# The head loop of a GroupNorm + attention kernel, rolled or written out

## What is computed

```python
def _gn(v, G=32, eps=1e-5):
    g = v.reshape(B_, G, C_ // G, H_, W_)
    m = jnp.mean(g, axis=(2, 3, 4), keepdims=True)
    s = jnp.var(g, axis=(2, 3, 4), keepdims=True)
    return ((g - m) / jnp.sqrt(s + eps)).reshape(v.shape)

def attention(x, Wq, Wk, Wv, Wp):            # HEADS = 12, dh = 64, N = H * W = 1024
    q, k, v = (jnp.einsum('oc,bchw->bohw', W, x).reshape(B, 12, 64, N) for W in (Wq, Wk, Wv))
    attn = jax.nn.softmax(jnp.einsum('bhdn,bhdm->bhnm', q, k) / 8, axis=-1)
    out = jnp.einsum('bhnm,bhdm->bhdn', attn, v).reshape(B, C, H, W)
    return jnp.einsum('oc,bchw->bohw', Wp, out)

x = x + attention(_gn(x), Wq, Wk, Wv, Wp)
```

## Time and profile before

| | |
|---|---|
| median of 3 runs | 3445.78 us (3442.05 to 3448.36) |
| the profiled execution | 3443.71 us |
| its span, first to last instruction | 3441.9 us |
| mean granted TensorE clock | 0.994 of full speed |
| instructions in the profile | 51849 |

### The profile page before, as it was taken

The page is one execution under the profiler, slowest core; times in us unless marked ns, Lnnn a source line. Parts: engine busy times, 40 slices in busy tenths (PEclk is TensorE's granted clock), DMA queues, the critical chain, the costliest instruction groups (busy, mean ns, idle before and its releaser), DMA issues.

```text
span 3441.9 us, 51849 instructions
## 1 busy us (share of the span) xinstructions
PE 3363.1 (98%) x18656; PEld 2257.7 (66%) x18656; DVE 1480.4 (43%) x1980; ACT 1116.3 (32%) x1992; POOL 1848.6 (54%) x795
## 2 busy tenths in 40 slices
PE   6999999999999979999999999999999999999999
PEld 5898888889888855445555555555555555555557
DVE  5332333233233145555444454444544545444431
ACT  3111111111111115554444444434444434444441
POOL 4000000000000029998888888888888888888883
PEclk9999999999999989999999999999999999999999
DMA  6332433423243332334434434434344334344434
GB/s 213 113 138 97 146 114 136 146 104 136 100 143 110 109 148 87 124 117 154 160 115 154 143 107 160 155 130 157 115 160 160 114 134 148 124 160 135 148 106 178
DMA packets 246840, 464.52 MB, mean 135 GB/s; under 512 B 47584, under 2 KB 97632, under 8 KB 245344
## 3 DMA queue, kind: packets, MB, share of 16 engines
q1 hardware_dynamic: 246624, 461.66, 38.7%
HBM read 260.11 MB, written 200.67 MB: 134 GB/s over the span
## 4 chain that ended last, share of the span: by engine, by line
PE 59%; issue 2%; DMA 1%; DVE 1%; SPq 1%; ACT 0%; POOL 0%; ACTq 0%; DVEq 0%; POOLq 0%
PE psum L754 20%; PE psum L767 19%; PE psum L786 10%; PE psum L737 7%; PE psum L849 1%; PE psum L777 1%; DVE half_max L930 1%; DMA out<-y 1%; DMA top<-turned 0%; ACT p_all L883 0%; SPq L570 0%; DMA k<-k_parts 0%; DVE flipped L940 0%; POOL sums L710 0%; DMA compact<-total 0%
## 5 line engine op out<-in xcount | busy, mean ns | idle before, releaser
L710 POOL TENSOR_TENSOR sums<-sums,p_all 128x1024 f32<-128x1024 f32 x576 | 1354.1, 2384 | 71.5 <-ACT p_all L883 71.3
L930 DVE TENSOR_REDUCE half_max<-psum 128x2 f32<-128x1024 f32 x768 | 939.5, 1225 | 645.7 <-PE psum L737 641.1
L883 ACT ACTIVATE p_all<-psum 128x512 f32<-128x512 f32 x1536 | 793.3, 602 | 919.6 <-PE psum L754 882.4
L767 PE MATMUL psum<-p_all,v 128*64 128x512 f32 x3072 | 743.4, 605 | 0.0
L754 PE MATMUL psum<-q,k 64*128 64x512 f32 x4608 | 667.4, 394 | 8.3 <-DMA top<-turned 5.8
L718 POOL TENSOR_TENSOR wp<-sums,wp 128x1536 fp32r<-128x1536 f32 x1 | 3.4, 3445 | 1177.6 <-ACT wp L916 1177.6
L754 PEld LDWEIGHTS psum<-q,k 64*128 64x128 f32 x4608 | 426.1, 185 | 120.3 <-ACT p_all L883 33.1
L240 PE MATMUL psum<-xn_hi,w_hi 128*128 128x512 f32 x1128 | 440.4, 390 | 7.0 <-DVE stage L377 7.0
L240 PE MATMUL psum<-xn_hi,w_lo 128*128 128x512 f32 x1128 | 439.5, 390 | 0.0
L240 PE MATMUL psum<-xn_lo,w_hi 128*128 128x512 f32 x1128 | 439.5, 390 | 0.0
L290 ACT CAST stage<-psum 128x512 fp32r<-128x512 f32 x192 | 112.6, 588 | 968.0 <-PE psum L240 962.5
(11 more groups left out here) (75 smaller groups left out, 2350.7 us busy)
## 6 DMA issues: line engine op xcount, KB each, us to landing
q_parts<-stage SPq DMA_DIRECT2D x192, 256.0 KB, 2.2
k_parts<-stage SPq DMA_DIRECT2D x192, 256.0 KB, 2.3
q<-q_parts SPq DMA_DIRECT2D x48, 1024.0 KB, 6.8
k<-k_parts SPq DMA_DIRECT2D x48, 1024.0 KB, 8.9
a<-o_parts SPq DMA_DIRECT2D x84, 512.0 KB, 7.9
v_rows<-stage SPq DMA_DIRECT2D x128, 192.0 KB, 2.1
v<-v_rows SPq DMA_DIRECT2D x48, 512.0 KB, 4.2
recip_all<-recip_rows SPq DMA_DIRECT2D x96, 256.0 KB, 3.8
```

What stands on the lines that cost most here:

```text
L710: pool.tensor_tensor(sums[:, m % 2, i, :], first, p_all[:, i, n, :], ALU.add).then_inc(added, 1)
L767: mm = pe.matmul(heads[part, h, :], v[:, e, t, part], p_all[:, i, (m * MT + t) % EXPS, cols], start=(t == 0), stop=(t == MT - 1))
L883: act.activation(p_all[:, i, (m * MT + t) % EXPS, h * BANK:(h + 1) * BANK], psum[:, SCORE_BANKS[2 * h + i], :], ACT.Exp, scale=SCALE).then ...
L930: dve.tensor_reduce(half_max[:, :, t, h], of, AX.X, ALU.max, negate=True).then_inc(max_done, 1)
```

## The change

Both places that run the pairs lose the hardware loop, and all 48 pairs are written out, on all engines. In the pairs 12 to 41 p becomes a number, as it is already in the others; each engine's program for them becomes five times as long. The loads, the stores, the matmuls, their order and their buffers are the same.

```diff
@@ -410,7 +410,6 @@
     BODY = KT
     SHIFT = 2
     LAG = KT + SHIFT
-    PEELED = 2 * BODY
     SCALE = float(DH) ** -0.5
@@ -514,12 +513,7 @@
 
         def all_pairs(eng, pair):
 
-            for p in range(PEELED):
-                pair(p, p % BODY, None)
-            with eng.Fori(PEELED // BODY, NP // BODY - 1) as u:
-                for m in range(BODY):
-                    pair(u * BODY + m, m, u)
-            for p in range(NP - BODY, NP):
+            for p in range(NP):
                 pair(p, p % BODY, None)
 
         def at_least(p, n):
@@ -652,12 +646,7 @@
             sp.wait_ge(set_done, SETS)
             maxima(0, 0)
             sp.wait_ge(wp_lo_done, len(wp_raw))
-            for p in range(PEELED):
-                pair(p, p % BODY, p // KT)
-            with sp.Fori(PEELED // BODY, B - 1) as b:
-                for m in range(BODY):
-                    pair(b * KT + m, m, b)
-            for p in range(NP - BODY, NP):
+            for p in range(NP):
                 pair(p, p % BODY, p // KT)
```

## The result

The changed kernel takes 3438.94 us (median of 22 runs, 3436.77 to 3440.63), the kernel before 3445.68 us (22 runs, 3441.52 to 3451.07). The ratio is 0.998 with a 95% interval of 0.9973 to 0.9986. That is 6.7 us less, just inside the bound of 0.2%, and the runs are closer together: 3.9 us from the lowest to the highest, where the kernel before has 9.5. The profiled execution took 3439.11 us with a span of 3437.3, 4.6 us less than the one before.

The account below looks back on a forecast made before the run. TensorE (PE), busy 98% of the span, was taken to bound the kernel. -8.25 + 3.0 = -5.25 us gave 3438.5 from the profiled 3443.71; with half of the median's extra 2.1 us, 3439.5 us, range 3433.5 to 3444.5.

Parts of the forecast that it names:

- Term 1: Pairs 12 to 41: the loop's four jumps back go, all of their cost on PE's path, -8.25 us.
- Term 2: ScalarE's exponents: the loop's quicker waits are lost, 0.10 us a pair over 30 pairs, +3.0 us (bounds +2.1 and +3.6).
- Term 3: Instruction queues: fetching the written-out code is not more than the loop's and costs nothing further.
- The half of 2.1 us: Median over profiled run: 2.1 us, some perhaps jump stalls that go as well; half was taken as saved.
- (a): Rival, the loop's jumps: larger in ordinary runs, 11.6 us, so -8.6 us and faster by over 0.2%; chance 0.36.
- (b): Rival, block boundaries on PE or SP: reading code in a line stalls, +18.6 us, 3457 us, slower; chance 0.05.
- (c): Rival, the jumps' place in the batch: jumps cost next to nothing, stalls stay, +3.0 us, 3446.7 us; chance 0.04.

Follow-up runs that it names:

- experiment 1: The changed kernel, but with TensorE alone keeping the loop and the other engines written out: 3444.45 us, ratio 1.0002 to the kernel before.
- experiment 2: The changed kernel, but with SyncE alone keeping the loop and the other engines written out: 3440.3 us, ratio 0.9992 to the kernel before.
- experiment 3: The kernel before with 24 pairs written out ahead of the loop in place of 12, so two jumps instead of four: 3440.08 us, ratio 0.999.
- changed_again: The changed kernel as it is, run again in a later batch as a yardstick: 3438.54 us, ratio 0.998 to the kernel before.
- project_straight: The changed kernel with the projection phase written out as well, so no loop is left: 3438.81 us, ratio 0.9981 to the kernel before.
- experiment 7: The changed kernel with the projection phase's loop at two batches per turn (3451.34 us, ratio 1.0022), or with that phase written out (3438.81 us, ratio 0.9981).

## Why the prediction was right

**Term 1** (the jumps, 8.25 us, all on PE's path) held in both its parts, and the runs separate them: PE's own jump 5.6 us in four pieces (experiment 1), SP's jump through the q and k loads, the store of y and the gathers, 0.7 us in that profile and 2.1 in the kernel before (experiment 2). Halving the jumps halved the pieces (experiment 3). The 0.7 us that the term put down to slower matmuls behind a pause is not shown by itself: with TensorE's jumps alone the 30 pairs take 1357.73 us, 5.80 more than in the changed kernel, which is its pieces of 5.6 and 0.2 more.

**Term 2** was mis-sized a little: 45.05 to 44.95 us a pair was forecast, +3.0 us; measured 45.06, +3.4 (1351.93 - 1348.5), inside its bounds of 2.1 and 3.6. Its cause, read from one product and one exponent, is confirmed from four sides: moving one wait brings 44.99 back in the written-out code, moving it makes the loop slower, keeping only ScalarE's loop gives 44.98, and the idle time ahead of line 743 shows it (3.2, 0.7 with ScalarE looped). That cause is 2.3 to 2.5 of the 3.4 us (1351.93 less 1349.67 or 1349.43). The rest, about 1 us or 0.03 a pair, no experiment brought back, and its cause stays open.

**Term 3** (transfer of the code costs nothing) held, and more than held: 64 blocks instead of 78.

**The sum.** Forecast -5.25 from profile to profile, measured 3443.71 - 3439.11 = -4.60; over the 30 pairs alone it is 1356.75 - 1351.93 = -4.82, 0.43 short, which is term 2. Forecast for the median 3439.5, measured 3438.94. The half of 2.1 us that I gave to stalls in ordinary runs was too little: the medians are 6.7 us apart in the kernels' own runs, and 4.8 in the batch of `changed_again` (3443.3 - 3438.54). So what the change is worth varies with the runs of the kernel before, where the changed kernel stays (3438.94, 3438.54). That the median came out within 0.6 us of the forecast is in part luck: the saving from profile to profile was forecast 0.65 us too large, and what the median adds to it, 1.05 us, should have been 2.1.

**The rivals.** (a), larger jumps, needed 9.9 us of them with 3.0 us for term 2, and 10.3 with the 3.4 that were measured; 6.7 + 3.4 = 10.1 is what the kernels' own runs give, 4.8 + 3.4 = 8.2 the later batch. The result is on the forecast's side of the bound by less than 0.2 us, which is luck as well, and the interval 0.9973 to 0.9986 holds the bound of 0.998. (b), stalls at block boundaries, did not come: the ticks of the changed kernel are 45.04 to 45.07 us apart from pair 9 to pair 46. (c), a cheap jump and stalls of the place, is ruled out by the changed kernel, which has no idle time at those places, by experiment 3, and by the branches of 3.4 to 3.8 us. For it spoke the Trainium skill's 51 and 108 ns for a branch (Advanced Engine Details and Errata, Control Flow Timing). PE's compare-and-branch takes 0.08 us here when it does not jump and 0.21 to 0.24 us when it jumps to code at hand, which costs no idle time; where the target has to be fetched the figures are too small by a factor of thirty and more.

## What to carry to other kernels

Ask of a hardware loop whether its body is still held when it jumps back: instruction transfers that stop inside the loop say yes, and then writing it out gains nothing (project_straight); where they went on, each jump cost the engine that sets the pace an idle piece, and the queue of transfers some 6 us of lateness that surfaced elsewhere. The branch instruction on the loop's line tells it as well: 0.2 us against 3.4 to 3.8 on PE. When two versions of a loop body exist in one kernel, their periods give the price of the change before it is made, in both directions. Of several waits ahead of one instruction, look which stands on the instruction itself: with constants it was the one written first, with registers the last, and it should be the one that ends last; here that was worth 3.8 us of the 8.6 between the kernel before and the best version.

## What was not expected

The two-batch loop cost 12.8 us for two jumps, against 1.4 us a jump in the attention phase. The batches tell where it went (PE's product of the variance, once a batch):

```profile
264.87 0.27 PE L198 MATMUL psum<-spread,avg 128*128 128x1 f32 x1 [1.17 <-DVE spread L338]
414.73 0.27 PE L198 MATMUL psum<-spread,avg 128*128 128x1 f32 x1 [1.17 <-DVE spread L338]
569.56 0.27 PE L198 MATMUL psum<-spread,avg 128*128 128x1 f32 x1 [1.16 <-DVE spread L338]
719.40 0.27 PE L198 MATMUL psum<-spread,avg 128*128 128x1 f32 x1 [1.17 <-DVE spread L338]
875.58 0.27 PE L198 MATMUL psum<-spread,avg 128*128 128x1 f32 x1 [1.16 <-DVE spread L338]
```

149.86 and 149.84 us without a jump, 154.83 and 156.18 with one: 4.97 and 6.33 us. Only 5.8 us of these 11.3 are idle pieces of PE. Most of the rest is clock: behind the pause the 512-column matmuls take 0.63 us instead of 0.39 (the timeline of experiment 7), and the stretches of that kernel show the granted clock (the column before the DMA share), the first three at the first jump and the last at the second:

```profile
492.00:495.00 3.00, 2.46 (x6) 1.97 (x7) 0.00 (x0) 0.00 (x0) 0.00 (x0) 0.62 0.04 11
495.00:500.00 5.00, 5.00 (x21) 4.01 (x21) 0.95 (x2) 1.30 (x2) 0.00 (x0) 0.89 0.00 0
500.00:510.00 10.00, 10.00 (x46) 8.29 (x45) 4.48 (x8) 2.60 (x4) 0.00 (x0) 1.00 0.40 150
...
796.00:804.00 8.00, 6.67 (x17) 5.26 (x18) 0.00 (x0) 0.00 (x0) 0.00 (x0) 0.57 0.05 13
```

PE stood for 0.51 and 2.32 us, the clock went to the lower of its levels (1.2 GHz) for part of the next 8 us and came back to 2.4 GHz while PE worked on. The clock that was missing is 0.38 x 3 + 0.11 x 5 = 1.7 us at the first jump and 0.43 x 8 = 3.4 at the second, where PE still stood for 0.8 us of the lower clock; what is left, some 4.7 us, is most of the 5.5. At the four jumps of the attention loop, with pieces of 1.2 to 1.6 us, the clock stayed at 1.00; the first of them:

```profile
2010.00:2024.00 14.00, 12.80 (x65) 6.62 (x66) 6.15 (x10) 3.98 (x7) 12.58 (x6) 1.00 0.21 81
```

The pause is longer here than there though the branch is not (3.36 us against 3.4 to 3.8). PE comes back after 0.51 us, makes one product and stops again, and in that second pause, 489.8 to 492.5 us, a further block of code is transferred:

```profile
q8 instruction: 1, 0.02, 2.2%
```

It lands at 491.17 and PE goes on at 492.54, 1.37 us later; the block before it landed at 488.07 and the branch ended at 489.44, 1.37 us later as well. That this jump needs two blocks, one after the other, is read from these times and was not tried by moving the body. The other 1.5 us of the 12.8 were not traced to the end; PE's one wait for the staging of the first groups, ahead of this loop, is 8.2 us in this profile and 7.8 in `changed_again`'s.
